# Sixteen float32 products in column pieces of 64 and 32 take the place of eighteen zero products ahead of the last experts

## The reference

```python
    x = x + _L1_ffn_ref(_layernorm(x, axis=-1)[None], L1_ffn_Wr, L1_ffn_br, L1_ffn_W1, ...)[0]
...
        router_logits = xf @ Wr + br
        topk_logits, topk_idx = jax.lax.top_k(router_logits, TOP_K)        # TOP_K = 1, E = 8
        topk_gates = jax.nn.softmax(topk_logits, axis=1)
            for e in range(E):
                h = jax.nn.relu(xf @ W1[e] + b1[e])                        # 512 -> 256
                oe = h @ W2[e] + b2[e]                                     # 256 -> 512
                out = out + jnp.where(idx_k == e, gate_k * oe, 0.0)
```

## Time and profile before

| | us |
|---|---|
| three runs | 1220.07, 1220.42, 1222.42 |
| median | 1220.42 |
| the profiled execution, its span and so its own time | 1220.4 |
| TensorE busy in it | 1052.0 |
| VectorE busy | 778.0 |
| the batch of 22 zero products in the chain that ended last | 6.87 |

### The profile page before, as it was taken

The page is one execution under the profiler, slowest core; times in us unless marked ns, Lnnn a source line. Parts: engine busy times, 40 slices in busy tenths (PEclk is TensorE's granted clock), DMA queues, the critical chain, the costliest instruction groups (busy, mean ns, idle before and its releaser), DMA issues. The chain is left out here.

```text
span 1220.4 us, 17917 instructions
## 1 busy us (share of the span) xinstructions
PE 1052.0 (86%) x5617; PEld 744.6 (61%) x5622; DVE 778.0 (64%) x1724; ACT 524.2 (43%) x752; POOL 625.3 (51%) x503
## 2 busy tenths in 40 slices
PE   3999899989599999999298799888898888777897
PEld 1454577778477777777055488787773434433575
DVE  6988578628233333332495889996368777787855
ACT  2234544231111111111133478889537776766323
POOL 1000458302557555543410587999478777685242
PEclk9999899855599999999589799999989999989899
DMA  3000003044388999992510111211012111172551
GB/s 117 1 0 1 1 1 137 2 170 151 132 285 296 301 302 307 303 306 94 182 35 1 37 45 43 87 53 36 9 39 69 36 53 35 37 242 72 179 173 42
DMA packets 107987, 134.57 MB, mean 110 GB/s; under 512 B 30240, under 2 KB 76040, under 8 KB 107792
## 3 DMA queue, kind: packets, MB, share of 16 engines
q1 hardware_dynamic: 92720, 112.68, 28.4%
q0 software_dynamic: 15200, 21.04, 5.3%
HBM read 135.03 MB, written 27.45 MB: 133 GB/s over the span
## 5 line engine op out<-in xcount | busy, mean ns | idle before, releaser
L2347 POOL TENSOR_TENSOR am<-CT,qb 128x1024 f32<-128x1024 f32 x128 | 302.2, 2385 | 29.5 <-ACT PT L2376 17.4
L2369 ACT ACTIVATE PS<-adb,ab 128x1024 f32<-128x1024 f32 x128 | 143.1, 1118 | 89.4 <-DVE am L2474 88.2
L2474 DVE TENSOR_TENSOR am<-PS,am 128x1024 f32<-128x1024 f32 x128 | 156.4, 1222 | 37.3 <-ACT PS L2369 30.2
L2468 DVE CUSTOM_DVE_ANT_0 masked<-PS,mask 128x1024 f32<-128x1024 f32 x128 | 156.2, 1220 | 32.4 <-issue 30.6
L2580 PE MATMUL PS<-PT,h 128*65 128x512 f32 x256 | 122.8, 611 | 36.6 <-ACT PT L2376 25.1
L1232 DVE COPY yo<-PS 128x512 f32<-128x512 f32 x64 | 44.3, 691 | 168.5 <-PE PS L1170 163.1
L2567 PE MATMUL PS<-h,PT 128*128 128x129 f32 x1024 | 128.0, 283 | 22.0 <-ACT PT L2376 12.2
L2376 ACT ACTIVATE PT<-am,as 128x1024 f32<-128x1024 f32 x128 | 145.2, 1134 | 0.3 <-DVE am L2474 0.3
L2567 PEld LDWEIGHTS PS<-h,PT 128*128 128x128 f32 x1024 | 121.1, 196 | 30.5 <-issue 18.2
L1197 ACT ACTIVATE hT<-PS,b1T 128x128 f32<-128x128 f32 x128 | 40.0, 363 | 214.8 <-PE PS L1162 195.7
L1162 PE MATMUL PS<-xgT,w1r 128*128 128x128 f32 x1024 | 125.8, 276 | 0.0
(11 more groups left out here) (426 smaller groups left out, 1777.9 us busy)
## 6 DMA issues: line engine op xcount, KB each, us to landing
w2r<-in_L_ffn_W SPq DMA_DIRECT2D x64, 512.0 KB
w1r<-in_L_ffn_W SPq DMA_DIRECT2D x64, 512.0 KB
adb<-a_scratch SPq DMA_DIRECT2D x16, 512.0 KB, 4.0
qb<-q_scratch SPq DMA_DIRECT2D x14, 512.0 KB, 3.8
wc<-in_L_gnn_W SPq DMA_DIRECT2D x4, 1024.0 KB, 9.2
w1x<-in_L_ffn_W SPq DMA_DIRECT2D x2, 2048.0 KB, 11.0
w2x<-in_L_ffn_W SPq DMA_DIRECT2D x2, 2048.0 KB, 9.3
w1x<-in_L_ffn_W SPq DMA_DIRECT2D x7, 512.0 KB, 5.4
```

The lines of the kernel that those rows point to most:

```text
L2347: pool.tensor_tensor(am[:, k % RING, :], CT[:, s, :], qb[:, hd % 2, :], ALU.add).then_inc(s_sum, 1)
L2369: act.activation(RELU, adb[:, hd % 2, :], ACT.Relu, bias=ab[:, s, hd:hd + 1]).then_inc(s_relu, 1)
L2468: dve.tensor_tensor_reduce(masked[:], wide(row_bank(hd)), mask[:, t, :], 1.0, -3.0e38, ALU.subtract, ALU.max, mrow[:, hd % 2, t:t + 1]).th ...
L2474: dve.tensor_tensor(am[:, k % RING, :], RELU, am[:, k % RING, :], ALU.add).then_inc(s_all, 1)
```

## The change

Four of the 22 zero products stay. The other eighteen are replaced by `narrow(pe, 64, 4)` and `narrow(pe, 32, 2)`: float32 products whose weights are 64 or 32 columns of the identity matrix and whose moving operand is 512 columns of the experts' first weights, already in SBUF. The piece of columns that starts at `at` writes the PSUM partitions from `at` on, so the pieces of one round together fill 128 partitions of one bank. That makes 4 x 2 products of 64 columns and 2 x 4 of 32. Their results, in banks 0 and 1, are read by nobody. No wait, transfer or instruction of another engine is added or removed.

```diff
             def zeros(self, pe, n):
                 for _ in range(n):
                     pe.matmul(PS[:, 0, :], onesb[:], zerob[:], start=True, stop=True)
 
+            def narrow(self, pe, columns, n):
+                for i in range(n):
+                    for at in range(0, P, columns):
+                        pe.matmul(PS[at:at + columns, i % 2, :], ident[:, at:at + columns],
+                                  self.w1x[:, at // 32 % 4, 0:2, :].rearrange("p k h -> p (k h)"), start=True, stop=True)
...
                 pe.wait_ge(self.s_w1[0], 16)
                 pe.wait_ge(self.s_w1[1], 16)
-                self.zeros(pe, 22)
+                self.zeros(pe, 4)
+                self.narrow(pe, 64, 4)
+                self.narrow(pe, 32, 2)
                 turn(0)
```

## The result

| | runs | median us | range us |
|---|---|---|---|
| before | 12 | 1220.55 | 1218.87 to 1222.49 |
| changed | 12 | 1224.62 | 1221.58 to 1228.70 |

The ratio is 1.0026 (95% interval 1.0014 to 1.0038), +1.7 to +4.6 us: slower, as forecast, and the median lies 0.5 us from the 1225.1 of the forecast. The way there is another one than the forecast took. One correction to the arithmetic: a run's device time is 1.8 us more than its span (1225.37 against 1223.6 in the changed kernel's profiled execution). So the profiled execution of before, with a span of 1220.4, took about 1222.2 us and was not the median run, as the table of the time before has it. The sum should have been made against the median, 1220.4 + 4.7, and not against a span; the two happened to be equal.

What follows compares the result with a forecast made beforehand. The prediction took TensorE's batch of zero products, which ends last before the first transposes, as the bound. Pieces ending at 1152.8 instead of 1148.07 add 4.7 us to 1220.4, giving 1225.1 us, range 1220.9 to 1231.5.

Steps and rivals of the forecast that it cites:

- 1220.4 + 4.7: Whole kernel: profiled execution of before plus the shift of the first transpose by a longer batch, 1225.1 us.
- The batch bounds the transposes: Before the first transposes: zero products end last, about 1.5 us after VectorE's first block, so lengthening the batch delays the experts.
- 32 records, 0.43 us each at clock 1.00 and 0.86 at 0.50: In the batch: sixteen float32 products are two records each, whatever their weight columns.
- Products are then issued strictly in order, and each adds one record's time instead of two.: Half overlap in the batch: the next piece's first record starts with this one's second; +4.7 us, chance 0.44.
- pieces in pairs or quartets: Sign in the batch's profile: pieces running so, or one by one, would make the prediction wrong.
- 13.3 x 0.48 us: In the batch: products left after the clock's rise, each one record plus uncovered load, 6.4 us.
- the two last records of 0.43: In the batch: second record of the last piece, at the change from 64 to 32 and at the end, 0.9 us.
- 0.05 us of uncovered load: In the batch: part of each weight load added to 0.43, giving 0.48 us a product at clock 1.00.
- The drain at a change of width: In the batch, from 64 to 32 columns: changing tiling mode drains the engine, so both last records count, 2 x 0.43.
- The clock: In the batch: rises from 0.50 to 1.00 at 1145.5, 2.6 us after the pieces begin; rival without rise 1234, 0.08.
- Pass-through: Behind the batch: TensorE's 0.99 us wait for ScalarE could swallow up to 0.99 us of the shift; none counted.
- the full overlap: Rival in the batch: all pieces of a round run together, 12 records, +1.3 us, 1221.7 us; chance 0.20.

Runs made afterwards that it cites:

- piece by piece: Changed kernel with the same sixteen products reordered, all rounds of one piece of columns, then all of the next; ratio to before 1.0048 (1.0029 to 1.0067).
- full width: Changed kernel with six float32 products of all 128 identity columns instead of the column pieces; ratios to before 1.0007 and, in a second set, 1.0016.
- long pair: Changed kernel with 96 column pieces (24 rounds of 64, 12 of 32), and its partner with 36 products of 128 columns; ratios to before 1.0200 and 1.0208.
- depth: Order of "piece by piece", with two rounds of 64 columns and four of 32; a single execution of 1230.05 us, no ratio.
- long pieces: Changed kernel with 24 rounds of 64 columns and 12 of 32, 96 products; ratio to before 1.0200 (1.0183 to 1.0218).
- four zero products: Changed kernel with both narrow lines taken out, nothing in place of the other eighteen zero products; ratio to before 1.0005 (0.9988 to 1.0021).
- 15 zero products: Kernel before with 15 zero products instead of 22; ratio to before 1.0013 (0.9994 to 1.0033).
- one place: Changed kernel with all pieces writing the PSUM partitions from 0 on, same sixteen products; ratio to before 1.0065 (1.0043 to 1.0087).

## Why the forecast was right, and where its steps were not

- **The batch bounds the transposes.** Right for the profiled execution: they follow the pieces at once, and the first block was ready at about 1148.7, 3 us before. Where the clock is high, the block, 5.4 us after the batch's start, and not the 4.75 us of zero products would be what before waits for; the forecast did not see that case.
- **32 records, 0.43 us each at clock 1.00 and 0.86 at 0.50.** Right, in all kernels, for 64, 32 and 128 columns. The row behind the forecast's 592 ns for 65 columns, of the kernel before:

```profile
L2580 PE MATMUL PS<-PT,h x256: 590/592/1095, 916.7 to 1126.6; 128*65 128x512 f32 x128
```

- **"Products are then issued strictly in order, and each adds one record's time instead of two."** This step failed, and by the forecast's own test, pieces in pairs or quartets, its mechanism was wrong. The second record of a piece does not keep the next piece waiting. What the runs show instead: the list is handed out in order to the column groups, each group works through its own records one after another, and about four records of a group, the running one among them, are held at a time. In the changed kernel a piece's neighbours in the list are other groups, so nothing is held up, and a round costs two records' time with two pieces and with four. The term of 13.3 x 0.48 us and the two last records of 0.43 go with it: 12 steps, not 16 and 2.
- **0.05 us of uncovered load.** Measured nothing: steps of 0.43 with loads of 0.14 us inside. The Trainium skill's "TensorE: Matmul & The Clock Gate", Part 3, says three things that bear on this. Products in different column groups run together: the trace agrees, with loads two and four at a time. Loads overlap products in flight only where row groups differ: not so here, since loads of 0.14 us for the same 128 rows lie inside running records. Products start strictly in list order: not so here across column groups, since in "piece by piece" the second piece's first record starts with the fifth of the eight that stand ahead of it (1147.45). In both the measurement decides.
- **The drain at a change of width.** The first load of the new width is not taken ahead; it comes 0.95 us after the last load of the old one, and a change costs about 0.1 us, not a record's time. The Trainium skill's "TensorEngine Tiling (Array Packing)", Key Properties, says that a change of tiling mode drains the engine; the trace agrees, at that price.
- **The clock** rose at 1147.6, 2.5 us after the pieces began, where the forecast had 2.6, and the 32s kept it at 1.00. That holds for this execution; in the second profile it was at 1.00 through the whole batch.
- **Pass-through.** The wait of 0.99 us for ScalarE is gone in the profile after, and what lies behind the batch is 0.5 us shorter. The forecast named it and counted nothing. It is no rule: from the first transpose to the end the second and third profiles of the change take 75.2 us (1224.8 - 1149.59) and 76.5 us (1230.7 - 1154.18), and the full width, without pieces side by side, 76.9 us (1227.0 - 1150.13) in one profile and 72.2 (1221.0 - 1148.79) in the other.
- **The size.** The lengths of the batches give +1.0 to +1.6 us, the full overlap of the forecast (+1.3). The ratios of three sets are 1.0026, 1.0016 and 1.0028; their mean, weighted by the inverse squares of the intervals, is 1.0025 +- 0.0009, +1.9 to +4.1 us. So the forecast met the median although its batch was 3.1 us too long, which is luck, and 0.3 to 3 us of the measured time are not accounted for. An excess that grows with the pieces is excluded by the long pair. What is left would be one fixed cost behind the pieces; the last section has a candidate that is argued, not shown, and the cause stays open.

## What to carry to other kernels

Narrow float32 products are worth interleaving by column group, round by round: two of 64 columns or four of 32 cost one full-width product, and a list that gives one group more than about four records in a row loses that. A filler's price is its steps and not its number of products, and it counts only as far as it ends after the work that the next step waits for. Against a spread of 0.3 to 0.9% between executions of before, an effect of 0.1% is better read from the stage than from the total.

## What was not expected

Signals of finished products came late in some executions. In before, VectorE's first copy starts 0.64 us after the first transpose. In the three profiles of the changed kernel it starts 0.92, 2.40 and 4.36 us after it; the second and the third, each with its transposes and its copy in the timeline (which writes "remote" where it finds no sender near enough to the signal):

```profile
1149.59 1.09 PE L1873 MATMUL PS<-ident,xn 128*128 128x128 f32 x8
1151.99 0.69 DVE L2056 COPY xnT<-PS 128x512 f32<-128x512 f32 x1 [2.97 <-PE PS L1873]
```

```profile
1154.18 1.09 PE L1873 MATMUL PS<-ident,xn 128*128 128x128 f32 x8
1158.54 0.69 DVE L2056 COPY xnT<-PS 128x512 f32<-128x512 f32 x1 [7.05 <-remote]
```

The first block's transposes themselves take 0.66 us. That it is the signal and not VectorE shows in the semaphore events of the second trace: the transposes end at 1150.24, their signal is there at 1151.97, and the copy starts 0.02 us later. In the third the wait costs more than its length: TensorE has nothing to do from 1155.28 to 1159.29, and then its clock is low for a stretch (a window of that execution, columns as in the earlier trace rows):

```profile
1160.50:1163.80 3.30, 3.30 (x18) 3.30 (x17) 3.06 (x13) 0.63 (x2) 0.00 (x0) 0.50 0.02 5
```

"Piece by piece" and "depth" show 2.0 and 1.4 us in this place, the long pieces none (0.69), and of the kernels without pieces side by side none is late here (1.15 us behind four zero products, where the transposes run at the low clock and take as long). Those have such waits elsewhere, 1.72 us ahead of line 1885 in the full width and 2.17 us with 15 zero products, as before had 0.99.

The traces show what these waits have in common. GpSimd gathers eight blocks one after another; the last of these rows in before and in the third profile of the change:

```profile
1152.40 1.07 POOL L1715 DMA_INDIRECT xg<-xs_scratch,x_picked  x1 [0.30 <-issue]
1156.25 0.99 POOL L1715 DMA_INDIRECT xg<-xs_scratch,x_picked  x1 [0.30 <-issue]
```

In before, the late `hTx` starts at 1154.47, 1.0 us after that row ends; in the third profile the late copy starts 1.3 us after it. In all eleven profiles in which the first experts fall among the gathers, some reader of TensorE's signals is held in this way until 1.0 to 1.4 us after the last gather; in the three whose transposes come after the gathers (one place, and the two long ones) the first copy follows within 0.7 us. So the lateness goes with the gathers, in kernels with pieces and without, though no run moves the gathers, and the cause is not shown. What differs is the place: the first copy, where nothing hides the wait, is late in all five such profiles with pieces side by side (by only 0.2 us in the first of the change) and in none of the six without. That could fill the gap in the size, but these are single executions, and no run here shows why pieces would do it.
